# Two recurrent layers on one core: key blocks paired anew, row maxima sent through two queues, output division and values moved within a turn

## The chip, the cores and the metric

The kernel runs on one core of one Trainium2 chip. The metric is the device time of one launch in microseconds (us), lower is better. Each kernel is run several times; the median and the span of the runs are given.

## What is computed

The reference takes x of shape (4, 512, 512) and applies two gated layers. Cut to what matters here:

```python
xn = _layernorm(x)
s = _L0_attn_ref(xn, wq, wk, wv, wo)        # causal attention, 32 query heads of 16, 8 key heads, rope
g = _silu(_L0_ffn_ref(xn, ...))             # 2 of 8 experts: mean of relu(x W_e + b_e) of the chosen two
x = x + s * g
xn = _layernorm(x)
s = _L1_attn_ref(xn, ...)                   # S4: a 512-tap kernel from 64 states, causal convolution
g = _silu(_L1_ffn_ref(xn, ...))             # a linear layer with block-scaled weights
return x + s * g
```

The attention is a softmax over the keys up to each query: scores = q k / 4, masked above the diagonal, minus their maximum, exponentiated, times v, divided by the row's sum, then the product with `wo`.

## The kernel before, in words

The program has three stages, each written by hand in the order in which every engine runs it, with semaphores between the engines. Stage A (to about 105 us) normalizes, projects q, k and v, turns them and writes high and low parts of the turned q and k to HBM. Stage C (from about 671 us) is the second layer. The change lies in stage B, attention and experts together.

Stage B runs 32 **turns**, one for each pair (b, h) of 4 batches and 8 groups (a group is one key head with its four query heads). A turn works on two groups at once: the second pass of its own group, and the first pass of the next group.

- First pass, `scores_1` (L1358): scores with queries on the partitions, ten steps n of 512 columns or less in three banks. For each, VectorE adds the mask and takes the maximum of every row (`maxima`, L1179). Step n of `scores_1` waits until the maxima of step n-3 are taken. After the tenth step VectorE writes the negated maxima as two parts (`maxima_parts`, L1192 and L1194), TensorE turns them (`turn_maxima`, L1393), VectorE copies them out of the bank (`maxima_rows`, L1202), and SyncE sends them with two DMAs into rows of `qt` beside the queries (`maximum_rows`, L1085), one for each half of the heads (s = 0, 1).
- Second pass, `scores_2` (L1380 and L1383): scores with keys on the partitions, the maximum subtracted by those rows. The causal triangle of 4 x 4 blocks of 128 has ten blocks (j, t), key block j against query block t. They go two at a time, for both halves of the heads, so ten steps. Where the two blocks of a pair share the key block, one matmul of 512 columns does both (L1380); otherwise there are two of 256 columns with different weights (L1383). ScalarE exponentiates each step (`exps`, L1283) from one of two banks, so step n waits for the exponential of step n-2. Step 0 waits for the rows of maxima in `qt`. GpSimd masks the diagonal blocks (`select`, L1103).
- `values` (L1407): key block j times v, in four quarters j = 0 to 3 of 8 matmuls each. Quarter j needs all exponentials of the blocks of j.
- The division: `rows_of` (L1212) turns the outputs on VectorE, which needs all four quarters; `normalise` (L1217, L1221) divides; every second turn `pair_rows` (L1229) turns them back for the projection.
- Between these, TensorE does the experts' tiles (`expert`, L1422 turns the gathered rows, L1434 and L1437 multiply) and the output projection of the batch before (`project`, L1450). Five **bursts** make a turn: a burst is steps n and n+1 of both passes. What follows them is in four pieces, `filler(0)` to `filler(3)`: a quarter each of a projection, of a second tile, or of a tile that is done late in the turn.

A table of tiles for each turn (MIDDLE, FIRST, LAST) says which tiles run in it. In turns h = 0 to 3 of batches 1 to 3 the fillers are a projection (I call these projection turns); in turns with two tiles they are the second one; in six turns from 180 us on (229, 324, 355, 450, 481 and 576 us) the only tile is done late in the fillers, so the bursts have no expert work between them (late turns).

VectorE's order in a turn is: the ten maxima, with the division of the group before behind maxima 1, 3 and 5 (`finish`); `maxima_parts`; `dve_s4`, pieces of the second layer's taps (L545 and others); `maxima_rows`; in the first two turns the routing of tokens to experts (`dve_route`, `dve_tokens`), whose result the first gather of rows (L1116) waits for. ScalarE's is: exponentials, the tile's copy (`expert_x`, L1290) and relu (`expert_y`, L1296), and the copy of the projected tile (`projected`, L1273) at the end of the turn. SyncE's is: the tile's store (L1516), `maximum_rows`, in odd turns the twelve loads of the next two groups (`load_stacks`, L1077 and L1078), more stores. After the last turn SyncE loads what stage C needs (`sp_c`, from L1585), and TensorE works out the taps (`pe_taps`, L650) in the fillers of turn (3, 7).

## Time and profile before

| | us |
|---|---|
| median of 3 runs | 762.63 (761.85 to 764.82) |
| the profiled execution, its own time | 762.54 |
| its span in the profile | 760.8 |
| outside the span | 1.7 |
| TensorE busy | 681.8 (90%) |
| VectorE busy | 531.4 (70%) |
| ScalarE busy | 303.0 (40%) |
| GpSimd busy | 251.9 (33%) |

The span is the profiled program from its first instruction to its last. A busy share is a sum over the three stages. Waits are read from a timeline: each row gives start and length in us, the engine, the line of the kernel, what is written and read, how many instructions were merged (xN), and in brackets the idle time of the engine before it with what ended it. The granted clock is TensorE's, 1.00 for 2.4 GHz and 0.50 for 1.2 GHz.

### The profile page before, as it was taken

How to read it: one execution, taken by the hardware profiler on the slowest of the kernel's cores; microseconds unless marked ns; L12 is line 12 of the kernel's file. 1: busy time of each engine (PE TensorE's matmuls, PEld its weight loads, DVE VectorE, ACT ScalarE, POOL GpSimd, SP SyncE). 2: the span in 40 equal slices, each digit the busy share in tenths (PEclk: the TensorE clock that was granted, in tenths of full speed). 3: DMA queues.
4: the chain of work that ended last, by engine and by line, in shares of the span. 5: the costliest groups of instructions: out<-in, count | busy, mean ns of one | idle time of the engine just before them, and what ended most of it. 6: DMA issues, size and time to landing. Idle time of an engine off the chain costs nothing. (4 is left out here: it accounts for less than half of the span.)

```text
span 760.8 us, 12565 instructions
## 1 busy us (share of the span) xinstructions
PE 681.8 (90%) x3653; PEld 377.5 (50%) x3679; DVE 531.4 (70%) x1775; ACT 303.0 (40%) x553; POOL 251.9 (33%) x419
## 2 busy tenths in 40 slices
PE   3999956749999999999999999999999978869997
PEld 2888843334444443444443444444444433358886
DVE  4799878877757666676665776657766573359994
ACT  4344313323435443355433444344443432235442
POOL 2765521352232322222231222322222214446630
PEclk9999975558999999999999999999998997879999
DMA  7487877851726425154362432624415218648851
GB/s 228 145 271 266 266 185 175 218 91 31 132 71 120 89 60 105 42 95 87 62 132 59 78 75 47 123 75 98 80 41 96 67 45 279 135 79 191 207 137 69
DMA packets 52813, 92.25 MB, mean 121 GB/s; under 512 B 7800, under 2 KB 20664, under 8 KB 52752
## 3 DMA queue, kind: packets, MB, share of 16 engines
q1 hardware_dynamic: 40800, 64.21, 35.5%
q0 software_dynamic: 6704, 18.62, 10.9%
q10 hardware_dynamic: 5248, 8.69, 3.6%
q8 instruction: 29, 0.48, 0.3%
q14 instruction: 32, 0.26, 0.1%
HBM read 61.53 MB, written 29.43 MB: 120 GB/s over the span
## 5 line engine op out<-in xcount | busy, mean ns | idle before, releaser
L1179 DVE CUSTOM_DVE_ANT_0 bank<-bank,cst 128x384 f32<-128x384 f32 (+3 forms) x512 | 236.3, 518 | 142.2 <-PE bank L1358 140.0
L1283 ACT ACTIVATE arena<-bank 128x512 f32<-128x512 f32 x320 | 176.3, 602 | 126.8 <-PE bank L1380 85.1
L1103 POOL TENSOR_SCALAR_AFFINE_SELECT arena<-arena 128x512 f32<-128x512 f32 x128 | 81.6, 637 | 360.7 <-ACT arena L1283 360.6
L1437 PE MATMUL bank<-w_e,arena 128*128 x312 | 158.0, 617 | 4.6 <-issue 2.6
L1358 PE MATMUL bank<-kt,qt 48*128 48x384 f32 (+3 forms) x512 | 136.6, 370 | 13.2 <-DVE arena L1179 11.4
L1358 PEld LDWEIGHTS bank<-kt,qt 48*128 48x128 f32 x512 | 82.2, 208 | 113.0 <-DVE arena L1179 84.3
L1407 PE MATMUL bank<-arena 128*32 128x512 f32 (+3 forms) x1024 | 103.1, 502 | 0.0
L1380 PE MATMUL bank<-qt,kt 50*128 50x512 f32 x192 | 81.2, 525 | 14.2 <-DMA qt<-arena 10.5
L1437 PEld LDWEIGHTS bank<-w_e,arena 128*128 128x128 f32 x312 | 51.9, 190 | 55.2 <-issue 54.1
L1179 DVE DVE_READ_ACCUMULATOR2_ANT arena<- 128x1 f32 x512 | 71.9, 140 | 0.0
L1296 ACT ACTIVATE arena<-bank 128x512 f32<-128x512 f32 x39 | 23.3, 597 | 114.1 <-PE bank L1437 114.1
L1450 PE MATMUL bank<-w_proj,arena 128*128 128x512 f32 x128 | 64.2, 635 | 4.1 <-DVE arena L631 4.1
L1383 PE MATMUL bank<-qt,kt 50*128 50x256 f32 x256 | 57.9, 351 | 0.2 <-ACT arena L1283 0.2
L1380 PEld LDWEIGHTS bank<-qt,kt 50*128 50x128 f32 x192 | 34.7, 197 | 28.8 <-DMA qt<-arena 18.3
L1116 POOL DMA_INDIRECT arena<-xn_rows,arena x39 | 38.8, 994 | 29.1 <-issue 20.7
L836 PE MATMUL bank<-proj_high,xh 128*128 128x512 f32 (+1 forms) x128 | 46.9, 367 | 0.0
L836 PE MATMUL bank<-proj_high,xl 128*128 128x512 f32 (+1 forms) x128 | 44.3, 346 | 0.0
L836 PE MATMUL bank<-proj_low,xh 128*128 128x512 f32 (+1 forms) x128 | 44.2, 345 | 0.0
L1273 ACT COPY s_tok<-bank 128x512 f32<-128x512 f32 x16 | 9.4, 586 | 84.3 <-PE bank L1450 84.3
L1383 PEld LDWEIGHTS bank<-qt,kt 50*128 50x128 f32 x256 | 41.4, 217 | 2.6 <-issue 1.7
L698 POOL TENSOR_TENSOR s_tok<-arena 128x256 f32<-128x256 f32 (+1 forms) x64 | 33.9, 562 | 22.8 <-DVE arena L454 22.8
L1450 PEld LDWEIGHTS bank<-w_proj,arena 128*128 128x128 f32 x128 | 23.2, 197 | 35.1 <-issue 30.2
(162 smaller groups left out, 983.1 us busy)
## 6 DMA issues: line engine op xcount, KB each, us to landing
qt<-turned_parts SPq DMA_DIRECT2D x96, 128.0 KB, 4.9
turned_parts<-qk_parts SPq DMA_DIRECT2D x8, 1280.0 KB, 6.9
expert_rows<-arena SPq DMA_DIRECT2D x39, 256.0 KB, 2.0
w_e<-in_L_ffn_W_e ACTq DMA_DIRECT2D x8, 1024.0 KB, 7.2
kt<-turned_parts SPq DMA_DIRECT2D x96, 64.0 KB, 4.8
arena<-in_L_attn_x SPq DMA_DIRECT2D x16, 256.0 KB, 4.4
xn_rows<-arena SPq DMA_DIRECT2D x16, 256.0 KB, 2.8
w_e<-in_L_attn_x SPq DMA_DIRECT2D x16, 256.0 KB, 3.7
```

The costliest lines, as they stand in the source:

```text
L698: i = g.tensor_tensor(o[:, :, :, c, :], xc[:, :, :, c, :], xs[:, :, :, 1 - c, :], op)
L836: i = t.matmul(out[u % 2][:, 0:n], x[:, u % 2, k, :], w[part][:, k, :], start=(k == 0 and x is xh and part == 0), stop=(k == KB - 1 and pa ...
L1103: g.affine_select(out=diag, in_=diag, compare_op=ALU.is_ge, fill=0.0, base=0, pattern=[[0, 2], [0, HALF], [1, P]], channel_multiplier=-1). ...
L1116: e.indirect_dma_start(xg[:, m % 2, :], None, xn_d, bass.IndirectOffsetOnAxis(ap=tok_b[:, m % 2, :], axis=0))\
L1179: i = v.tensor_tensor_reduce(out=part, in0=part, in1=const("mask")[:, S - w:], scale=1.0, scalar=LOWEST, op0=ALU.add, op1=ALU.max, accum_o ...
L1283: a.activation(pt[:, s, 2 * i:2 * i + 2].rearrange("p c r q -> p (c r q)"), bank[2 + s], ACT.Exp, scale=HD ** -0.5)\
L1358: i = t.matmul(S1_BANK[n % 3][:, at:at + w], qt[rows, h // 2 % 2, h % 2, x if r is None else r, q * P:w], kt[rows, h // 2 % 2, h % 2, 0:w] ...
L1380: i = t.matmul(bank[2 + s], keys(j), queries[:, q:q + 2], start=True, stop=True)
L1383: i = t.matmul(bank[2 + s][:, x * HALF * P:(x + 1) * HALF * P], keys(j), queries[:, q], start=(x == 0), stop=True, skip_group_check=True)
L1407: i = t.matmul(bank[4][VW * r:VW * (r + 1), j * P:], vb[:, j, h, :], pt[:, r // HALF, at:at + TPB - j, r % HALF, :], start=(j == 0), stop= ...
L1437: i = t.matmul(bank[7], xgt[:, k, :], w_e[:, ex[b * MPB + m], k, :], start=False, stop=(k == KB - 1))
L1450: i = t.matmul(bank[to_bank or 7], ot[:, (b * PAIRS + k) % (PAIRS + 1), u, :], wo[:, k, :], start=(k == 0), stop=(k == KB - 1))
```

## The change

Four edits, all in stage B.

1. The ten blocks are paired by a table (`PAIRED`) in place of their order. Four of five pairs now share a key block; only ((1,3),(3,3)) does not. The exponentials write to the two places of a pair with a stride. Quarter 1 of the values now needs the last pair's exponentials, quarter 2 those of the fourth pair.
2. `maximum_rows` sends one half from SyncE and the other from ScalarE, where it stands behind the ten exponentials of the turn.
3. On VectorE, `maxima_rows` stands ahead of `dve_s4`, and the division of a group stands at the end of its own turn, behind both, in place of between the next turn's maxima. In turn (0, 0) it stands ahead of the routing, in turn (0, 1) behind it.
4. On TensorE, quarters 1 to 3 of the values stand together behind `filler(0)`, `filler(1)` and the turning of the maxima. The second tile's transposes move from behind the fifth burst to behind the fourth, its copy on ScalarE from behind the tenth exponential to behind the eighth.

```diff
+PAIRED = [((0, 0), (0, 1)), ((0, 2), (0, 3)), ((1, 1), (1, 2)), ((2, 2), (2, 3)), ((1, 3), (3, 3))]
...
-        VALUES_AFTER = [max(n for n in range(NJ) if (j, TPB - 1) in BLOCKS[n // 2 * 2:n // 2 * 2 + 2]) + 1 for j in range(TPB)]
+        VALUES_AFTER = [max(n for n in range(NJ) for t in range(j, TPB) if (j, t) in PAIRED[n // 2]) + 1 for j in range(TPB)]
...
-        def maximum_rows(e, b, h):
+        def maximum_rows(e, b, h, s):
 
             e.wait_ge(b_me, nth_of(1, b, h, 1))
-            for s in range(2):
-                at = 64 * s + ROWS
-                e.dma_start(qt[at:at + 2, h // 2 % 2, h % 2].bitcast(F32), m_rows[8 * TPB // 2 * s:8 * TPB // 2 * (s + 1), :]).then_inc(b_mr, 16)
+            at = 64 * s + ROWS
+            e.dma_start(qt[at:at + 2, h // 2 % 2, h % 2].bitcast(F32), m_rows[8 * TPB // 2 * s:8 * TPB // 2 * (s + 1), :]).then_inc(b_mr, 16)
...
                     for n in range(NJ):
                         if h + 1 < NG or more:
                             maxima(e, *next_group(b, h, 1), n)
-                        finish(b, h - 1, n)
                     if h + 1 < NG or more:
                         maxima_parts(e, st, *next_group(b, h, 1))
-                    dve_s4(e, st, b, h)
                     if h + 1 < NG or more:
                         maxima_rows(e, *next_group(b, h, 1))
+                    dve_s4(e, st, b, h)
+                    if due(b) or h != 1:
+                        finish(b, h)
                     if not due(b) and h < 2:
                         dve_route(e, st, h)
                     if not due(b) and h == 1:
                         dve_tokens(e, st)
+                        finish(b, h)
...
-                if due(at := nth_of(4, b, h, BLOCKS[2 * i + 1][0] - 3)):
+                if due(at := nth_of(4, b, h, PAIRED[i][1][0] - 3)):
                     e.wait_ge(b_pv, at)
-                a.activation(pt[:, s, 2 * i:2 * i + 2].rearrange("p c r q -> p (c r q)"), bank[2 + s], ACT.Exp, scale=HD ** -0.5)\
-                    .then_inc(b_e, 1)
+                first, second = (BLOCKS.index(block) for block in PAIRED[i])
+                a.activation(pt[:, s, first:second + 1:second - first].rearrange("p c r q -> p c (r q)"),
+                             bank[2 + s].rearrange("p (c x) -> p c x", c=2), ACT.Exp, scale=HD ** -0.5).then_inc(b_e, 1)
...
-                    if second is not None:
-                        expert_x(b, second)
+                        if n == Y_AT and second is not None:
+                            expert_x(b, second)
+                    if h + 1 < NG or more:
+                        maximum_rows(e, *next_group(b, h, 1), 1)
...
-                    if second is not None:
-                        expert(b, h, second, 0)
-                    values(b, h, 1)
+                            if second is not None:
+                                expert(b, h, second, 0)
                     filler(0)
+                    filler(1)
                     if following:
                         turn_maxima(*following)
-                    values(b, h, 2)
-                    values(b, h, 3)
-                    for k in range(1, 4):
-                        filler(k)
+                    for j in range(1, TPB):
+                        values(b, h, j)
+                    filler(2)
+                    filler(3)
```

The order of the instructions shows two of the moves. On TensorE, the end of turn (2, 0) before: the last scores of the second pass are `bank<-qt,kt`, the values `bank<-arena`, the projection `bank<-w_proj,arena`, the turned maxima `bank<-cst,m_parts`, the first pass `bank<-kt,qt`.

```order
L1383 MATMUL bank<-qt,kt 128x256 x2
L1407 MATMUL bank<-arena 32x384 x4
L1450 MATMUL bank<-w_proj,arena 128x512
L1393 MATMUL bank<-cst,m_parts 32x128
L1407 MATMUL bank<-arena 32x256 x4
L1407 MATMUL bank<-arena 32x128 x4
L1450 MATMUL bank<-w_proj,arena 128x512 x3
L1358 MATMUL bank<-kt,qt 128x512
```

The same place in the changed kernel:

```order
L1380 MATMUL bank<-qt,kt 128x256 x2
L1447 MATMUL bank<-w_proj,arena 128x512 x2
L1390 MATMUL bank<-cst,m_parts 32x128
L1404 MATMUL bank<-arena 32x384 x4
L1404 MATMUL bank<-arena 32x256 x4
L1404 MATMUL bank<-arena 32x128 x4
L1447 MATMUL bank<-w_proj,arena 128x512 x2
L1355 MATMUL bank<-kt,qt 128x512
```

Quarter 1 of the values went behind the turned maxima, and a second quarter of the projection came ahead of them. On VectorE, the end of turn (2, 3) before: `m_parts` are the maxima's parts, `arena<-arena 128x64` is `dve_s4`, `COPY arena<-bank 32x128` is `maxima_rows`, and the `ISA` rows are the next turn's maxima.

```order
L1194 SCALAR_TENSOR_TENSOR m_parts<-arena,m_parts 128x2x8
L545 TENSOR_TENSOR arena<-arena 128x64 x3
L570 RECIPROCAL arena<-arena 128x64
L545 TENSOR_TENSOR arena<-arena 128x64 x2
L1202 COPY arena<-bank 32x128
L1179 ISA bank,arena<-bank,cst 128x512
```

The same place in the changed kernel:

```order
L1194 SCALAR_TENSOR_TENSOR m_parts<-arena,m_parts 128x2x8
L1202 COPY arena<-bank 32x128
L546 TENSOR_TENSOR arena<-arena 128x64 x3
L571 RECIPROCAL arena<-arena 128x64
L546 TENSOR_TENSOR arena<-arena 128x64 x2
L1212 STREAM_TRANSPOSE arena<-bank 128x512
L1217 RECIPROCAL arena<-arena 128x16
L1221 TENSOR_TENSOR arena<-arena 128x16x16
L1229 STREAM_TRANSPOSE arena<-arena 128x512
L1179 ISA bank,arena<-bank,cst 128x512
```

The copy of the maxima comes ahead of the second layer's work, and the whole division of the turn's group stands ahead of the next turn's first maxima.

## Rows read from the trace of the kernel before

**Rows 1.** Timeline of TensorE, end of turn (2, 1), start of the next.

```profile
411.57 0.85 PE L1407 MATMUL bank<-arena 128*32 128x384 f32 x8
412.36 1.13 PE L1450 MATMUL bank<-w_proj,arena 128*128 128x512 f32 x2
413.64 0.28 PE L1393 MATMUL bank<-cst,m_parts 128*32 128x128 f32 x1 [0.16 <-DVE m_parts L1194]
413.85 0.86 PE L1407 MATMUL bank<-arena 128*32 128x256 f32 x16
414.64 2.84 PE L1450 MATMUL bank<-w_proj,arena 128*128 128x512 f32 x6
417.41 0.49 PE L1358 MATMUL bank<-kt,qt 48*128 48x512 f32 x1
418.58 0.60 PE L1380 MATMUL bank<-qt,kt 50*128 50x512 f32 x2 [0.67 <-DMA qt<-arena]
```

**Rows 2.** Timeline of SyncE's queue, ends of turns (2, 1) and (2, 3).

```profile
414.27 1.26 SPq L1085 DMA_DIRECT2D qt<-arena  x2
...
448.21 1.26 SPq L1085 DMA_DIRECT2D qt<-arena  x2
```

**Rows 3.** Waits of the second pass at L1380, both of TensorE's engines, 181 to 612 us.

```profile
  DMA qt<-arena: 13.5, 25
```

**Rows 4.** Timeline of TensorE, end of turn (2, 3), where `dve_s4` is long.

```profile
446.16 0.28 PE L1393 MATMUL bank<-cst,m_parts 128*32 128x128 f32 x1 [0.16 <-DVE m_parts L1194]
...
450.83 0.60 PE L1380 MATMUL bank<-qt,kt 50*128 50x512 f32 x2 [0.40 <-DMA qt<-arena]
```

**Rows 5.** Timeline of ScalarE, start of turn (2, 2).

```profile
417.52 0.58 ACT L1273 COPY s_tok<-bank 128x512 f32<-128x512 f32 x1 [4.94 <-PE bank L1450]
```

**Rows 6.** Timeline of TensorE, third and fourth burst of turn (2, 1), what follows each.

```profile
406.37 0.44 PE L1358 MATMUL bank<-kt,qt 48*128 48x384 f32 x1
...
407.08 1.12 PE L1437 MATMUL bank<-w_e,arena 128*128 x2
408.14 0.44 PE L1358 MATMUL bank<-kt,qt 48*128 48x384 f32 x1
...
408.85 1.06 PE L1407 MATMUL bank<-arena 128*32 128x512 f32 x8
```

**Rows 7.** Timeline of TensorE, late turn from 324 us.

```profile
329.65 0.44 PE L1358 MATMUL bank<-kt,qt 48*128 48x384 f32 x1 [0.47 <-DVE arena L1179]
...
330.09 1.73 PE L1407 MATMUL bank<-arena 128*32 128x512 f32 x8
```

**Rows 8.** Windows, right behind: length; busy PE, PEld, DVE, ACT, POOL; clock; DMA.

```profile
330.40:333.80 3.40, 3.40 (x24) 1.13 (x16) 3.27 (x16) 1.51 (x3) 0.64 (x1) 0.50 0.97 107
```

**Rows 9.** Timeline of VectorE, turn (0, 0): routing begins; the next maxima.

```profile
133.06 0.70 DVE L868 TENSOR_TENSOR arena<-arena 128x128 f32<-128x128 f32 x1
...
139.02 0.70 DVE L1179 CUSTOM_DVE_ANT_0 bank<-bank,cst 128x512 f32<-128x512 f32 x1
```

**Rows 10.** Timeline of TensorE, end of turn (0, 0), and turn (0, 2).

```profile
132.74 1.51 PE L1407 MATMUL bank<-arena 128*32 128x256 f32 x16
...
166.12 1.11 PE L1422 MATMUL bank<-cst,arena 128*128 128x128 f32 x4 [4.48 <-DMA arena<-xn_rows,arena]
```

**Rows 11.** Timeline of TensorE, turn (3, 7): second pass; taps.

```profile
627.15 0.67 PE L1380 MATMUL bank<-qt,kt 50*128 50x512 f32 x2 [4.05 <-DMA qt<-arena]
...
636.71 2.39 PE L650 MATMUL bank<-w_e,roots 128*128 128x512 f32 x4
```

**Rows 12.** Timeline of SyncE's queue: the load for the taps.

```profile
626.28 0.43 SPq L1585 DMA_DIRECT2D w_e<-in_dft  x1
```

**Rows 13.** DMA issues, KB each and median us to landing: the same load.

```profile
w_e<-in_dft SPq DMA_DIRECT2D x1, 2048.0 KB, 9.0
```

**Rows 14.** Timeline of VectorE: division of the last group, then stage C's scales.

```profile
639.95 0.72 DVE L1212 STREAM_TRANSPOSE arena<-bank 128x512 f32<-128x512 f32 x1 [14.02 <-PE bank L1407]
...
642.09 2.46 DVE L1674 TENSOR_TENSOR w_e<-w_e,arena 128x512 f32<-128x512 f32 x4
```

More of the change, by code:

```diff
@@ L1013, in build @@
         NLD = 2 * 3 * 2
-        SELECT_AFTER = [max(n for n in range(NJ) if (j, j) in BLOCKS[n // 2 * 2:n // 2 * 2 + 2]) + 1 for j in range(TPB)]
-        VALUES_AFTER = [max(n for n in range(NJ) if (j, TPB - 1) in BLOCKS[n // 2 * 2:n // 2 * 2 + 2]) + 1 for j in range(TPB)]
+        SELECT_AFTER = [max(n for n in range(NJ) if (j, j) in PAIRED[n // 2]) + 1 for j in range(TPB)]
+        VALUES_AFTER = [max(n for n in range(NJ) for t in range(j, TPB) if (j, t) in PAIRED[n // 2]) + 1 for j in range(TPB)]
         xb = bank[6].rearrange("p (k t) -> p k t", k=KB)
@@ L1229, in pair_rows, with finish @@
                 v.transpose(ot[:, (b * PAIRS + i) % (PAIRS + 1)].rearrange("p t f -> p (t f)"), o2.rearrange("p q c -> p (q c)")).then_inc(b_o2, 1)
-            def finish(b, h, n):
-                if h < 0 and not due(b):
-                    return
-                b, h = (b, h) if h >= 0 else (b - 1, NG - 1)
-                if n == ROWS_AT:
-                    rows_of(b, h)
-                if n == NORMALISE_AT:
-                    normalise(b, h)
-                if n == PAIR_AT and h % 2:
+            def finish(b, h):
+                rows_of(b, h)
+                normalise(b, h)
+                if h % 2:
                     pair_rows(b, h // 2)
@@ L1264, in dve_b @@
                 go(b, b + 1 < NB)
-            for n in (ROWS_AT, NORMALISE_AT, PAIR_AT):
-                finish(NB - 1, NG - 1, n)
             dve_scale(e)
@@ L1331, in build @@
         X_AT, Y_AT = 1, 7
-        ROWS_AT, NORMALISE_AT, PAIR_AT = 1, 3, 5
         def scores(e, n0, g1, g2):
@@ L1371, in scores_2 @@
             rows = slice(64 * s, 64 * s + ROWS + 2)
-            pair = BLOCKS[2 * i:2 * i + 2]
+            pair = PAIRED[i]
             queries = qt[rows, h // 2 % 2, h % 2].rearrange("p r (t q) -> p t r q", q=P)
@@ L1523, in go @@
                     if h + 1 < NG or more:
-                        maximum_rows(e, *next_group(b, h, 1))
+                        maximum_rows(e, *next_group(b, h, 1), 0)
                     if h % 2 and (h + 3 < NG or more):
@@ L1540, in go @@
                                  .then_inc(b_wo, 16)
-            maximum_rows(e, 0, 0)
+            for s in range(2):
+                maximum_rows(e, 0, 0, s)
             load_stacks(e, 0, 2)
```

## The prediction
> **What bounds the kernel now.** I read the shares first: TensorE is busy 90% of the span, VectorE 70%, ScalarE 40%. So I looked for what stops TensorE in stage B, 32 turns of about 16 us, with the timeline of one turn. The end of turn (2, 1) [rows 1] shows TensorE without a break except in two places. It waits 0.16 us for the maxima's parts before it turns them, and then, with the next turn's first-pass step issued at 417.41, it starts the second pass at 418.58, 1.17 us later, held by the DMA of the maxima's rows. A DMA that is not on any busy list therefore ends every turn. The chain to it is: turned maxima 413.64, two DMA issues of 0.63 us each from 414.27 [rows 2], landing and start at 418.58, which is 4.94 us behind the turned maxima, while TensorE has 3.77 us of work in between (413.64 to 417.41). The burst that holds the wait grows by all of it. Over 181 to 612 us this wait shows as 13.5 us of idle time in 25 of 27 turns [rows 3]. That is the prize and its bound.
>
> The wait has three parts. In turn (2, 3) the DMA issue comes 2.05 us behind the turned maxima (446.16 to 448.21) against 0.63 in turn (2, 1) [rows 1, 2, 4]: 1.42 us of `dve_s4` stands ahead of the copy. The second issue adds 0.63 us. From the end of the second issue, 449.47, to the start at 450.83 are 1.36 us of flight; in turn (2, 1), where the loads of the next stacks follow, the flight is 3.05 us (415.53 to 418.58).
>
> **Edit 3, first half: the copy ahead of `dve_s4`.** In six turns (2 and 3 of batches 1 and 2, 0 and 1 of batch 3) `dve_s4` delays the copy by about 1.4 us, in some others by less. In turn (2, 3) the second pass starts 0.9 us behind the first (0.49 of its step, 0.40 idle) [rows 1, 4]. 1.42 us earlier, it does not wait. Six times 0.9 is 5.4 us of the 13.5.
>
> **Edit 2: two queues.** Where the issue binds, 0.63 us go; where the engines are loaded and both land together, little. With quarter 1 moved, TensorE's work between turned maxima and next turn stays 3.7 to 3.8 us: 0.85 more for quarter 1, 0.94 less for a quarter of a projection (2.84 us for three) [rows 1]. So of the other 8.1 us I leave 0.8 us each in two turns with the longest waits, the one in rows 1 among them. ScalarE takes a floor: its copy at the start of a turn ends 0.69 us behind TensorE's first step (417.41 to 418.10) [rows 1, 5], and the first exponential can't start sooner. A second pass 0.1 us late costs nothing for that, so a tenth in 19 turns is not won. Sum of both edits: 13.5 - 1.6 - 1.9 = **10.0 us** won. Bounds: 13.5 if all goes, 5.4 if the second queue brings nothing. What ScalarE pays, one issue of 0.63 us a turn, lies in its idle time behind the tenth exponential (4.94 us before the copy of rows 5); nothing waits for it there. The late relu and the projected copy queue behind this wait, but need TensorE's last filler, 2 us later.
>
> The Trainium skill, page "DMA: Bandwidth & Descriptors", section "Issuing engines are not separate DMA queues", says that issuing from several engines saves the issue time alone, since all run on the same 16 engines. By it the flight of 3.05 us stays; that is the second rival.
>
> **Edit 4.** In projection turns, TensorE now has two projection quarters (some 1.9 us by rows 1, and about 0.2 for the change of operand) ahead of the turned maxima, where it had 0.85 + 1.13 and a wait. The turned maxima stay in place, at the end of the fifth burst plus 2.05; the wait and one change of operand go: 0.15 us in 12 turns, **1.8 us** (0 to 3). In turns with a second tile the transposes only move within TensorE's work, the copy still lands before its matmuls; I cost it at nothing, covered by the fifth burst (0.7 us), else 0.3 us a turn in 13 turns.
>
> **Edit 3, second half: the division.** Transpose, reciprocal, product and, in odd turns, the second transpose take 2.14 us (639.95 to 642.09), without the last 1.5 [rows 14]. They leave the maxima. That matters in the six late turns, where bursts two to four follow each other: the fourth waits 0.47 us for VectorE at 329.65, right ahead of the values at 330.09 [rows 7]. ScalarE is nearly as tight there, so I take 0.5 us a turn, **3.0 us** (1 to 6). The division now waits for quarter 3, which ends about 1.8 us behind the turned maxima, and must be done when the next first step is (another 2.4 us, a filler pair and the step): 2.14 fits. Where `dve_s4` and the numerators are long, in turns (0, 2) and (0, 3), it ends late; I take **1.3 us lost** (0 to 2).
>
> It costs in turn (0, 0). There the division stands ahead of the routing, which starts at 133.06 and ends at 139.02 [rows 9]. Quarters 1 to 3 run from 132.74 at half clock; quarters 2 and 3 take 1.5 us [rows 10], quarter 1 as much (equal at full clock, rows 1). So quarter 3 ends at 135.7, the division at 137.2, and the routing is 4.1 us late. The next maxima win 1.3 us back without a division among them. The chain goes on to the token lists and the gather that TensorE waits 4.48 us for at 166.12 [rows 10]: **2.8 us lost** (1.5 to 4).
>
> **Edit 1.** The fourth burst loses two matmuls of a half each. The third burst has the same first pass and whole matmuls already: 0.71 us from 406.37 to 407.08; the fourth: 0.71 us from 408.14 to 408.85 [rows 6]. So pairing is worth **nothing**; bounds 0 and 0.1 us a turn.
>
> **The end.** Turn (3, 7) waits 4.05 us for the rows behind the last `dve_s4` [rows 11]. That goes, but the taps come next: they need a load issued at 626.28 that takes 9.0 us [rows 12, 13]. The issue comes 2.1 us earlier at most, as it stands behind the last tile's relu, so it lands at 633.2. Then two tap quarters (2.3 us each at half clock) and three of values (1.5 to 3) run before the division: 639.3 to 640.8 against 639.95 [rows 11, 14]. **Nothing** won (2.7 won to 0.9 lost).
>
> **Sum.** -10.0 - 1.8 - 3.0 + 1.3 + 2.8 = -10.7. The profiled execution took 762.54 us, 0.1 under the median; 762.5 - 10.7 = **751.8 us**. All terms at their bounds give about 738 to 760.
>
> **The rivals.**
> - *The clock.* Behind each late turn's bursts the granted clock falls to 0.50 for 3.4 us or 6.8, six times; one of them is in [rows 8]. Values at half clock take 1.73 against 1.06 [rows 6, 7], and the burst and quarter 1 behind them lose as much: 1.5 to 2 us a fall. If shorter waits keep 2.4 GHz there, 8 us more: 744. For it: TensorE was idle in the bursts just before. Against: they stay limited by ScalarE.
> - *The engines, not the issue.* The rows land no earlier through two queues, by the flight of 3.05 us in rows 1. Then 13.5 falls to 5.4 us and 751.8 becomes 756.4.
> - *VectorE late at every turn.* The division, waiting for quarter 3 through the masks, ends behind the next turn's first step. The fourth first-pass step needs maximum 0, so I estimate that the first 0.4 us of lateness is free, about half a burst [rows 6]; each further us costs one in 31 turns. At 1 us late (1.2 us over my estimate) it costs 31 x 0.6 = 18 us: 770, slower. For it: the margin in odd turns is under 0.3 us. Against: all durations in it are measured, and the even turns have 1 us to spare without the second transpose.
> - *The end and the start go badly*, each at its bound, and the late turns win nothing: 759 to 761.
>
> **Chances.** Forecast 0.53, clock 0.17, engines 0.17, VectorE 0.07, the last 0.06. About 0.5%, 3.8 us, is what a measurement can tell. Faster: 0.85; same: 0.09; slower: 0.06. The range, 743 to 760, leaves out the slower case, and the far end of the clock's.
>
> **What would show it.** Right: the copy 0.3 us behind the turned maxima everywhere; one row DMA on each queue, 0.6 us each; second pass under 0.2 us behind the first step in most turns; the fourth burst 0.7 us as before; routing beginning near 137 us. Wrong: VectorE's division ending behind the next first step, or TensorE waiting for maxima in the second burst; rows landing 4.9 us behind the turned maxima still.

## The result and the profile after

| | before | after |
|---|---|---|
| median, us | 763.1 (761.85 to 764.82) | 774.14 (771.31 to 778.96) |
| profiled execution: own time, span | 762.54, 760.8 | 778.96, 777.2 |
| mean granted clock | 0.917 | 0.903 |

The changed kernel takes 1.0145 times as long, interval [1.0108, 1.0183]. The forecast was 751.8 us, with a range of 743 to 760 and 0.06 for slower. The profiled execution after is the longest of its four, so what is read from it is set against experiments that change one thing each. In what follows a ratio is to the kernel before as run beside it. The ratio of the run with the routing first leaves out two of its six executions, which were in a slower state of the chip, and so stands for 745 us where the median of all six is 749.05.

First, where the time went. The windows view, cut where the maxima are turned at the end of turn (0, 3) and at the end of turn (3, 5), the same two steps in both kernels; the columns are length, busy time (instructions) of PE, PEld, DVE, ACT and POOL, granted clock, DMA share and GB/s. Before:

```profile
0.00:193.21 193.21, 149.73 (x848) 107.24 (x850) 151.08 (x436) 64.38 (x119) 82.98 (x169) 0.81 0.66 186
193.21:603.33 410.12, 393.68 (x2155) 174.58 (x2176) 276.44 (x1088) 180.99 (x340) 106.69 (x175) 0.97 0.42 83
603.33:760.80 157.47, 138.39 (x654) 95.64 (x653) 103.85 (x253) 57.61 (x94) 62.19 (x75) 0.91 0.54 141
```

After:

```profile
0.00:196.30 196.30, 149.16 (x836) 107.35 (x836) 150.52 (x433) 64.43 (x119) 83.24 (x169) 0.82 0.65 183
196.30:619.66 423.36, 399.38 (x2125) 181.39 (x2124) 289.17 (x1088) 180.52 (x340) 109.00 (x175) 0.94 0.41 80
619.66:777.20 157.54, 137.83 (x657) 95.12 (x656) 105.88 (x254) 57.62 (x94) 61.71 (x75) 0.91 0.54 141
```

The end is unchanged (+0.1 us), the start lost 3.1, and the 26 turns between lost 13.2. There TensorE's matmuls stood idle for 24.0 us (423.36 - 399.38) against 16.4, and were busy 5.7 us longer although they were fewer; the granted clock was 0.94 against 0.97.

What ended the idle time, from the waits view of this stretch (total us, times, longest). Before, for matmuls alone:

```profile
PE bank L1380 <- DMA qt<-arena: 3.8, 8, 0.7
PE bank L1422 <- DMA arena<-xn_rows,arena: 0.5, 1, 0.5
```

After (L1377 is the second pass, L1419 the transposes of a tile's gathered rows):

```profile
PE bank L1377 <- DMA qt<-arena: 11.9, 11, 2.4
PE bank L1419 <- DMA arena<-xn_rows,arena: 10.0, 6, 2.3
```

[rows 3] has 13.5 us in 25 places for the first of these. It adds the waits of two queues of TensorE, 3.8 us of the matmuls in 8 places and 9.7 us of the weight loads that run ahead of them in 17. The 8 turns of the matmuls are among the 17 of the weight loads, so the same waits are in the sum twice; what TensorE lost to the rows before the change is 3.8 us in 8 turns.

By the matmuls' count the wait that the change was to remove grew threefold (by [rows 3]'s count, which has 16.0 us of weight loads more, it doubled), and a new one stands beside it: TensorE now waits for gathered rows. Of the 22.0 us of both, 20.1 follow the turned maxima of the 13 odd turns, where SyncE issues the stack loads, and 2.0 those of the 13 even turns. One place of each kind. First the end of turn (2, 3) of after, which answers to [rows 2, 4], on TensorE, then on SyncE's queue:

```profile
457.96 0.28 PE L1390 MATMUL bank<-cst,m_parts 128*32 128x128 f32 x1
458.18 1.50 PE L1404 MATMUL bank<-arena 128*32 128x384 f32 x24
459.61 1.99 PE L1447 MATMUL bank<-w_proj,arena 128*128 128x512 f32 x4
461.53 0.49 PE L1355 MATMUL bank<-kt,qt 48*128 48x512 f32 x1
463.91 0.60 PE L1377 MATMUL bank<-qt,kt 50*128 50x512 f32 x2 [1.89 <-DMA qt<-arena]
```

```profile
458.59 0.62 SPq L1085 DMA_DIRECT2D qt<-arena  x1
459.38 0.33 SPq L1078 DMA_DIRECT2D kt<-turned_parts  x1
459.74 0.62 SPq L1079 DMA_DIRECT2D qt<-turned_parts  x1
...
464.71 0.42 SPq L1079 DMA_DIRECT2D qt<-turned_parts  x1
```

Every step that the change controls went as meant: the copy is at once behind the turned maxima, the row DMA is issued 0.63 us behind them (ScalarE's half at 458.60), where [rows 2, 4] have 2.05 and then a second issue. But the second pass starts 5.95 us behind the turned maxima; before it was 4.67. From the row's issue to the start are 5.3 us. Right behind the row, SyncE issues the loads of the next stacks (`load_stacks`, every second turn), twelve of 64 and 128 KB, ten of them within these 5.3 us. They too start earlier than they did, since they queue behind the row: 1.4 us behind the turned maxima, where the same turn had 3.5 before (446.16 to 449.64) and turn (2, 1) had 2.1.

```profile
449.64 0.33 SPq L1077 DMA_DIRECT2D kt<-turned_parts  x1
```

The second kind, at the start of turn (2, 6), on TensorE and on GpSimd, which had issued the gather of these rows at 491.12, 0.6 us behind the turned maxima:

```profile
496.50 0.84 PE L1419 MATMUL bank<-cst,arena 128*128 128x128 f32 x4 [1.67 <-DMA arena<-xn_rows,arena]
```

```profile
491.12 1.20 POOL L1116 DMA_INDIRECT arena<-xn_rows,arena  x1 [0.75 <-POOL arena L1111]
```

The gather landed 5.3 us after its issue, at 496.46. In the kernel before, the same one was issued 0.1 us behind the turned maxima (477.64) and landed in 3.3 us. All six waits of this kind follow an odd turn, with the stack loads issued beside the gather, and these six gathers took 4.7 to 5.9 us.

What follows, by windows (columns as above): TensorE had full clock up to the wait, and behind it 1.2 GHz for 10.2 us, without a break in its work. Not all of that can be put to the wait: in the kernel before the clock fell in this turn too, for 3.4 us (487.4 to 490.8).

```profile
490.53:496.80 6.27, 4.60 (x37) 2.05 (x37) 4.54 (x11) 1.57 (x3) 3.01 (x4) 1.00 0.63 123
496.80:507.00 10.20, 10.20 (x40) 6.09 (x39) 6.52 (x30) 4.93 (x9) 2.11 (x5) 0.50 0.72 120
```

From these turned maxima to the next it took 17.2 us (490.53 to 507.71), and 14.6 in the kernel before:

```profile
477.56:492.16 14.60, 13.31 (x76) 6.10 (x76) 10.45 (x42) 6.53 (x12) 4.83 (x8) 0.88 0.78 136
```

In after's turn (3, 4), of the same kind, TensorE waited for nothing, and it took 12.1:

```profile
592.03:604.13 12.10, 12.10 (x76) 5.91 (x75) 10.65 (x41) 6.30 (x12) 3.90 (x6) 1.00 0.78 119
```

### The profile page after: what moved, and what is told of

It reads as the page before. It is cut to its first block and busy times, and to the rows that moved or that the text cites. A ratio compares the mean times of both kernels' runs of the same rounds, so it can differ in the third digit from the quotient of the medians.

```text
span 777.2 us, 12463 instructions
## 1 busy us (share of the span) xinstructions
PE 686.4 (88%) x3615; PEld 383.9 (49%) x3615; DVE 545.6 (70%) x1775; ACT 302.6 (39%) x553; POOL 253.9 (33%) x419
## 3 DMA queue, kind: packets, MB, share of 16 engines
q1 hardware_dynamic: 40242, 63.95, 34.2%
q0 software_dynamic: 6704, 18.62, 11.2%
## 5 line engine op out<-in xcount | busy, mean ns | idle before, releaser
L1434 PE MATMUL bank<-w_e,arena 128*128 x312 | 165.3, 642 | 0.0
L1355 PEld LDWEIGHTS bank<-kt,qt 48*128 48x128 f32 x512 | 84.2, 215 | 106.1 <-DVE arena L1179 58.0
L1377 PE MATMUL bank<-qt,kt 50*128 50x512 f32 x256 | 112.8, 531 | 16.0 <-DMA qt<-arena 13.6
L1404 PE MATMUL bank<-arena 128*32 128x512 f32 (+3 forms) x1024 | 92.6, 482 | 0.0
L1434 PEld LDWEIGHTS bank<-w_e,arena 128*128 128x128 f32 x312 | 56.1, 202 | 59.0 <-issue 56.2
L1377 PEld LDWEIGHTS bank<-qt,kt 50*128 50x128 f32 x256 | 48.3, 204 | 28.2 <-DMA qt<-arena 19.1
L1116 POOL DMA_INDIRECT arena<-xn_rows,arena x39 | 41.1, 1054 | 29.1 <-issue 20.8
L1404 PEld LDWEIGHTS bank<-arena 128*32 128x32 f32 x1024 | 27.7, 114 | 33.4 <-issue 25.5
L1212 DVE STREAM_TRANSPOSE arena<-bank 128x512 f32<-128x512 f32 x32 | 22.9, 717 | 26.3 <-PE bank L1404 25.5
L1419 PE MATMUL bank<-cst,arena 128*128 128x128 f32 x156 | 26.3, 293 | 15.1 <-DMA arena<-xn_rows,arena 15.0
```

The costliest lines, as they stand in the source:

```text
L1116: e.indirect_dma_start(xg[:, m % 2, :], None, xn_d, bass.IndirectOffsetOnAxis(ap=tok_b[:, m % 2, :], axis=0))\
L1355: i = t.matmul(S1_BANK[n % 3][:, at:at + w], qt[rows, h // 2 % 2, h % 2, x if r is None else r, q * P:w], kt[rows, h // 2 % 2, h % 2, 0:w] ...
L1377: i = t.matmul(bank[2 + s], keys(j), queries[:, q:q + 2], start=True, stop=True)
L1404: i = t.matmul(bank[4][VW * r:VW * (r + 1), j * P:], vb[:, j, h, :], pt[:, r // HALF, at:at + TPB - j, r % HALF, :], start=(j == 0), stop= ...
L1434: i = t.matmul(bank[7], xgt[:, k, :], w_e[:, ex[b * MPB + m], k, :], start=False, stop=(k == KB - 1))
```

## The experiments

**Theory L** after the first look: the loads of the stacks, released earlier, are in flight with the rows and the gathers, and delay both; TensorE stops, and its clock falls. **Rival Q**: the rows' two halves delay each other, or the second queue costs something. **Rival T**: the second tile's earlier place causes the waits for gathered rows, and these the loss. **Rival V**: VectorE's late division. In the first four expectations Q stands for L and Q together (the rows meet the loads, on ScalarE's queue above all).

### The changed kernel with both halves from SyncE

```diff
                     if h + 1 < NG or more:
-                        maximum_rows(e, *next_group(b, h, 1), 0)
+                        for s in range(2):
+                            maximum_rows(e, *next_group(b, h, 1), s)
```

and without ScalarE's issue.

> The changed kernel with both halves of the maxima's rows sent from SyncE again, ahead of the stack loads. Theory Q (the half on ScalarE's queue meets the stack loads, which now start 0.6 us sooner): in stack-loading turns the rows land within 3 to 4 us of the copy in place of 4.8 to 5.9, second pass late by 1 us at most, total 760 to 766. Theory T (the gathers are late since two ScalarE copies stand ahead of the last exponentials, and TensorE waits for their rows): total 770 to 775, the waits for gathered rows unchanged at about 15 us. Theory V (division at the turn's end holds up the first maxima): 772 to 776.

Measured: 783.19 us (777.4 to 784.95), ratio to before 1.0242 [1.0184, 1.0301]. All three forecasts were too low. The second queue is a gain of 7 to 9 us inside the changed kernel (the intervals of the two ratios just part), not its fault: rival Q falls.

### The changed kernel with the loads held behind the rows

```diff
                     if h % 2 and (h + 3 < NG or more):
+                        e.wait_ge(b_mr, nth_of(32, *next_group(b, h, 1), 32))
                         load_stacks(e, *next_group(b, h, 3))
```

> The changed kernel, two queues kept, but SyncE issues the stack loads only once both halves of the rows have landed. Theory Q: the rows land 2.0 to 2.4 us behind the copy in every turn and the gathers within 3.5 us of issue, waits for gathered rows fall from 15 us to under 3, total 750 to 758. Theory T: the rows as Q says, but X0 waits stay over 8 us, 764 to 770. Theory V: 770 or more.

Measured: **749.29 us** (744.18 to 754.22), ratio 0.9811 [0.9747, 0.9874]. One wait on SyncE turns 1.5% slower into 1.9% faster, and V falls. The same stretch, cut at the same steps, and its waits:

```profile
196.75:585.67 388.92, 383.38 (x2125) 173.71 (x2124) 288.21 (x1088) 179.05 (x340) 109.76 (x175) 0.99 0.43 88
```

```profile
PE bank L1377 <- DMA qt<-arena: 2.5, 10, 0.5
PE bank L1419 <- DMA arena<-xn_rows,arena: 0.5, 2, 0.3
```

Against after: 34.4 us shorter, of which 18.4 are idle time (24.0 to 5.5) and 16.0 the same 2125 matmuls in 383.4 us rather than 399.4. So the clock took nearly as much as the waits. The two traces overstate both: this one is of the shortest of four executions (744.18), that of after of the longest, and the medians are 24.9 us apart. That the clock has a part is clear without them: it was 0.903 to 0.913 in the four executions of after and 0.918 to 0.933 in these. The end of turn (2, 3) again, TensorE and SyncE's queue:

```profile
438.68 0.28 PE L1390 MATMUL bank<-cst,m_parts 128*32 128x128 f32 x1
...
443.05 0.60 PE L1377 MATMUL bank<-qt,kt 50*128 50x512 f32 x2 [0.32 <-DMA qt<-arena]
```

```profile
439.30 0.62 SPq L1085 DMA_DIRECT2D qt<-arena  x1
443.02 0.32 SPq L1078 DMA_DIRECT2D kt<-turned_parts  x1
```

From issue to start 3.75 us, against 5.3. SyncE's first load is now issued as soon as both halves have landed, so its time tells the landing, here 3.72 us after the row's issue. The DMA engines' share of those stretches, issue to start (first after, second this kernel; columns as in the windows above):

```profile
458.60:463.90 5.30, 3.42 (x29) 1.31 (x21) 4.30 (x12) 0.59 (x1) 0.96 (x1) 1.00 0.71 130
```

```profile
439.30:443.05 3.75, 3.43 (x30) 1.32 (x22) 3.44 (x10) 0.58 (x1) 0.96 (x1) 1.00 0.25 74
```

### The changed kernel with the second tile back in its old place

```diff
                         if n == Y_AT and first is not None and not late:
                             expert_y(b, first)
-                        if n == Y_AT and second is not None:
-                            expert_x(b, second)
+                    if second is not None:
+                        expert_x(b, second)
```

and on TensorE `expert(b, h, second, 0)` likewise, behind the fifth burst.

> The changed kernel with the second tile's transposes and copy at their old places (behind the fifth burst, behind the tenth exponential). Theory T: the two gathers of such turns go out 0.6 us sooner, waits for gathered rows fall from 15 us to 5, total 762 to 768. Theory Q: rows in the projection turns land as late as in the changed kernel, the gathers gain little, total 770 to 776. Theory V: 772 to 776.

Measured: 780.52 us (777.64 to 785.2), ratio 1.0226 [1.0167, 1.0285]. All forecasts were too low again. No wait for gathered rows is left, yet the kernel is no faster than after (6 us slower by the medians, with intervals that overlap): rival T falls. The waits of the second pass are longer still, and TensorE waits for the tile's copy:

```profile
PE bank L1377 <- DMA qt<-arena: 13.9, 6, 3.2
PE bank L1434 <- ACT arena L1286: 6.8, 9, 0.8
```

### The kernel before with two queues

The `maximum_rows` of the change, its second half issued by ScalarE behind `expert_x`, nothing else.

```diff
+                    if h + 1 < NG or more:
+                        maximum_rows(e, *next_group(b, h, 1), 1)
                     if late:
                         expert_y(b, first)
```

> The kernel before with the two queues alone. Theory Q: slower than before, 764 to 772, rows landing 4.8 to 5.9 us behind the copy in stack-loading turns. Theories T and V: a gain of 1 to 5 us, 758 to 762, since the issue of 0.6 us goes.

Measured: 767.98 us (766.51 to 770.24), ratio 1.0059 [1.001, 1.0108]. Alone, the second queue loses 4 us, just clear of noise. The loads, which stood behind both issues, now stand behind one.

### The kernel before with the loads held

The same wait ahead of `load_stacks` as above, in the kernel before.

```diff
+                        e.wait_ge(b_mr, nth_of(32, *next_group(b, h, 1), 32))
                         load_stacks(e, *next_group(b, h, 3))
```

> The kernel before, and SyncE waits for both landings of the maxima's rows before it issues the twelve stack loads of odd turns. Theory L (the stack loads, issued about 2.1 us behind the turned maxima, meet the rows in flight; in the kernel before that costs TensorE little more than 7 us, since its waits ahead of the next scores sum to 14.7 us over turns 4 to 30): with the loads held the waits fall to 8 to 10 us in sum, 755 to 761 us. Rival (holding the loads is worth some 25 us by itself in any kernel, as it was in the changed one, for a reason that has nothing to do with the change's earlier issues): 735 to 745 us. Rival (the loads then come too late for their own use, or nothing hangs on them): 763 to 770 us.

Measured: 760.95 us (758.12 to 766.24), ratio 0.998 [0.9948, 1.0013]. So the loads are nearly harmless there, and the 25 us in the changed kernel are a matter of the two together. At the end of turn (2, 3) the second pass starts 4.67 us behind the turned maxima with the loads held and without; at that of turn (2, 1), where the loads had followed 2.1 us behind them, it starts at 4.33 in place of 4.94. In the kernel before other things fill or end the same gap: the rows leave behind `dve_s4` and a second issue, and TensorE waits for VectorE as well.

```profile
PE bank L1358 <- DVE arena L1179: 3.5, 6, 0.8
PE bank L1380 <- DMA qt<-arena: 3.0, 8, 0.5
```

### Loads held, one queue

Both edits, on the changed kernel.

```diff
+                        for s in range(2):
+                            maximum_rows(e, *next_group(b, h, 1), s)
...
+                        e.wait_ge(b_mr, nth_of(32, *next_group(b, h, 1), 32))
```

> The changed kernel with the loads held behind the rows, and both halves of the rows issued by SyncE as before. By the changed kernel with loads held and two queues (749.3 us) and my term for the second queue (1.26 us of one issue in each of 31 turns, of which TensorE saw nearly all): theory Q (the second queue saves its 1.2 us a turn once the loads are out of its way): 30 to 40 us more than 749, of which the clock is a part, so 765 to 785 us if the rows wait for each other as they did in the one-queue run (30.2 us of waits); with the term alone, 27 turns x 0.7 us, 760 to 768 us. Rival (the whole loss was the loads, the queue of the rows matters little): 747 to 754 us.

Measured: 761.63 us (754.23 to 764.8), ratio 0.9951 [0.9914, 0.9988]. That is what the term alone would give. Against 749.3 the second queue is worth 12 us, and the loads held are worth 22 us with one queue too (783.2 to 761.6). The order within one queue is therefore not how the loads do harm: here the rows always stand ahead of them on the same queue. The second issue of 0.63 us shows as waits in 17 turns, 3.3 us more in sum than with two queues, and the rest of the 12 us is other idle time and clock:

```profile
PE bank L1375 <- DMA qt<-arena: 5.8, 17, 0.5
```

### Loads held, the division back between the maxima

```diff
                     for n in range(NJ):
                         if h + 1 < NG or more:
                             maxima(e, *next_group(b, h, 1), n)
+                        finish(b, h - 1, n)
```

with the `finish` of the kernel before.

> The changed kernel with the loads held, and the division of the outputs (rows, reciprocals, pairs) put back between the maxima of the next group, where the kernel before has it. Theory (the prediction's term: the division between the maxima cost 3.0 us in late turns and 1.8 us in projection turns, and something of the dve_s4 turns; with the loads held these terms are the gain): 754 to 760 us against 749.3. Rival (VectorE's place is free, since TensorE waits for the maxima only in the late turns): 748 to 752 us. Rival (the division behind the maxima delays the expert numerators more than it gains): under 747 us.

Measured: 755.49 us (752.89 to 759.68), ratio 0.9911 [0.988, 0.9942]: 6 us slower than with the division behind the maxima, as the theory had it. TensorE waits for VectorE again, which it did once, for 0.5 us, in the kernel with the loads held:

```profile
PE bank L1360 <- DVE arena L1179: 4.0, 6, 0.9
```

### The loads held longer

```diff
+                        e.wait_ge(b_e, nth_of(NJ, *next_group(b, h, 1), 4))
                         load_stacks(e, *next_group(b, h, 3))
```

> The changed kernel, with the twelve stack loads of odd turns held until the fourth exponential of the next turn is done, some 7 us behind the maxima, when the gathers of the second tile's rows have landed as well. Theory L (rows and gathers both pay for the loads beside them): gathers land within 4 us again, TensorE's waits for gathered rows fall below the 1.0 us of the run with loads held behind the rows, and the time is at or a little below it, 743 to 750 us. Rival (gathers aren't disturbed by loads, rows alone are): within 0.3% of 749.3. Rival (the loads collide with the next turn's gathers, weights or rows instead): 752 us or more, with waits at other places.

Measured: 770.33 us (767.55 to 773.55), ratio 1.0087 [1.0061, 1.0113]. The last rival was right. SyncE now stands in this wait while a store and the next turn's loads queue behind it, and the first pass waits for the stacks themselves:

```profile
PE bank L1355 <- DMA qt<-turned_parts: 8.6, 4, 2.7
```

So the loads have a window: behind the rows, but not 7 us behind the maxima.

### Loads held, the copy back behind `dve_s4`

```diff
+                    dve_s4(e, st, b, h)
                     if h + 1 < NG or more:
                         maxima_rows(e, *next_group(b, h, 1))
-                    dve_s4(e, st, b, h)
```

> The changed kernel with the loads held behind the rows, and the copy of the turned maxima put back behind the expert step dve_s4, as the kernel before has it. The term of the prediction: in six turns the copy stood 0.9 us or so behind dve_s4, 5.4 us in sum. Theory (the term was right): 749.3 + 4 to 6 us, 753 to 756 us. Rival (TensorE has other work in those turns, so the copy's place is free): 748 to 751 us. Rival (the wait stops TensorE and its clock falls, at more than the wait itself): 757 us or more.

Measured: 764.66 us (759.45 to 769.66), ratio 1.0029 [0.9999, 1.0059]: 15 us for the place of one copy of 0.28 us, which is the last rival's range. (`dve_s4` is the second layer's taps and no expert step.) It isn't only the six turns that I counted. A turn in which `dve_s4` is short, on VectorE, and what TensorE then does:

```profile
351.72 0.42 DVE L546 TENSOR_TENSOR w_proj<-w_proj 128x256 f32<-128x256 f32 x1
352.17 0.42 DVE L584 TENSOR_REDUCE arena<-w_proj 128x4 f32<-128x256 f32 x1
352.63 0.28 DVE L1202 COPY arena<-bank 32x128 f32<-32x128 f32 x1
```

```profile
356.32 0.60 PE L1377 MATMUL bank<-qt,kt 50*128 50x512 f32 x2 [0.41 <-DMA qt<-arena]
```

The copy comes 0.45 us later than behind the turned maxima, the row is issued at 352.94, and the second pass waits. Why so little matters so much is seen on SyncE's queue, where the first load tells the landing. End of turn (2, 5) with the copy in its new place, turned maxima at 468.56:

```profile
469.19 0.62 SPq L1085 DMA_DIRECT2D qt<-arena  x1
471.40 0.32 SPq L1078 DMA_DIRECT2D kt<-turned_parts  x1
```

With the copy put back, turned maxima at 474.97:

```profile
476.05 0.62 SPq L1085 DMA_DIRECT2D qt<-arena  x1
479.47 0.33 SPq L1078 DMA_DIRECT2D kt<-turned_parts  x1
```

Issued 0.45 us later, the rows land 1.65 us later, 4.50 behind the turned maxima in place of 2.85. In the 13 odd turns from (0, 3) to (3, 3), with the loads held and both edits in, the landing is 2.8 to 3.0 us behind the turned maxima in seven turns and 4.0 to 4.3 in six; with the copy back, or with one queue, it is 4.0 to 4.6 in all thirteen, although the issues lie between 0.6 and 2.1. Up to about 3.5 us a landing costs TensorE nothing, since it has work until then. What the rows wait for beyond their issue is not shown; the gather of a tile's rows is issued 0.6 us behind the turned maxima in all these turns, and lands at 4 to 5 us where the trace has it.

The waits in all are 7.2 us in 17 turns against 2.5 in 10, and TensorE's busy time for the same work grows from 383.4 to 395.3 us:

```profile
194.27:600.50 406.23, 395.25 (x2126) 179.04 (x2125) 290.45 (x1089) 180.14 (x340) 107.16 (x175) 0.97 0.42 84
```

### Loads held, the blocks paired as before

```diff
-PAIRED = [((0, 0), (0, 1)), ((0, 2), (0, 3)), ((1, 1), (1, 2)), ((2, 2), (2, 3)), ((1, 3), (3, 3))]
+PAIRED = [tuple(BLOCKS[n:n + 2]) for n in range(0, len(BLOCKS), 2)]
```

> The changed kernel with the loads held, and the score blocks paired as the kernel before pairs them (two of the five pairs with two keys, rather than one). Theory (bursts are bound by the exponentials that empty the banks, burst 4 took 0.71 us in both kernels, so the pairing is worth nothing): 748 to 751 us. Rival (one weight load and one start fewer in each of 64 bursts of 32 turns is worth 0.1 us each): 754 to 757 us. Rival (values 1 to 3 wait for later exponentials with the new order of blocks, so that the old one gains): 745 to 747 us.

Measured: 749.64 us (745.87 to 754.9), ratio 0.9835 [0.9791, 0.9878]. No difference within the 0.5% that these runs resolve: the pairing is worth nothing that can be measured. Its trace has 390.5 us of busy matmuls in the stretch (2178 of them) against 383.4.

### Loads held, routing ahead of the division in turn (0, 0)

```diff
                     if not due(b) and h < 2:
                         dve_route(e, st, h)
+                    if not due(b) and h == 0:
+                        finish(b, h)
```

> The changed kernel with the loads held, and in turn (0,0) the expert routing ahead of the division of the outputs, as in turn (0,1). The term of the prediction was +2.8 us for routing behind the division in turn (0,0). Theory (the term was right: the gathers and so the first expert rows come 2.5 us earlier): 746 to 747.5 us. Rival (the division then comes late for the values of the next turn, and gives it back): 749 to 752 us. Rival (the wait only moves, since the gathered rows bound that turn by their flight): 748.5 to 750 us.

Measured: 749.05 us (739.84 to 754.06), ratio 0.9769 [0.9712, 0.9825]. The times don't tell it from the kernel with the loads held; the ratios' intervals overlap. The trace shows the term, though: the first gathered rows' transposes start 34.2 us behind the maxima turned at the end of turn (0, 0) (133.16 to 167.31), 35.9 with the division first (134.43 to 170.29), and 33.7 in the kernel before.

```profile
167.31 1.12 PE L1421 MATMUL bank<-cst,arena 128*128 128x128 f32 x4 [4.42 <-DMA arena<-xn_rows,arena]
```

### Loads held, the second tile back

> The changed kernel with the loads held, and the second tile's transposes, their copy by ScalarE and so the next gather at the places of the kernel before. Theory (the tile's new place costs only where its gather meets the loads, which are now held; it takes nothing from the path otherwise): 748 to 752 us, with waits for gathered rows at 0. Rival (the new place brings the values 1 to 3 together and keeps TensorE's clock up): 755 to 762 us. Rival (the new place is still a loss, since gathers are issued 0.5 us later): 744 to 747 us.

The edit is that of the third experiment, on the kernel with the loads held. Measured: 754.85 us (753.03 to 756.62), ratio 0.9904 [0.9869, 0.994], at the lower edge of the first rival. The new place of the tile is a gain of some 6 us with the loads held, as it was with them free (774.1 against 780.5); each time the intervals just meet, so it is the two together that speak for it. What TensorE waits for with the tile back is the tile's copy, 6.8 us in 9 places in both kernels, and nowhere with the new place. With the tile back, holding the loads gains 26 us although no gathered row is ever waited for. So the rows of the maxima alone can carry the loss. How it divides between rows and gathers in the changed kernel itself isn't shown; its trace has 11.9 us of waits for the one and 10.0 for the other.

## Why the prediction was wrong

**What failed is one assumption under Edit 2 and Edit 3, that the flight stays.** I subtracted time from the issue of the rows and left their flight alone, 1.36 us in turn (2, 3) and 3.05 in turn (2, 1), "where the loads of the next stacks follow", with 0.8 us in two turns for the loads. But the loads follow in turn (2, 3) too, at 449.64; what differs is that they came late there. They are issued by the same engine right behind the row, so everything that makes the row earlier makes them earlier, and the work that covers the flight did not grow. From the end of the row's issue to the start, turn (2, 3) went from 1.36 us to 4.70. I asked of VectorE and ScalarE what queues behind a moved step, but not of SyncE, where the next instructions are those loads. The last of my signs of being wrong came, and worse than I had it: rows used 5.95 us behind the turned maxima. Nor does the flight stay with the loads held: issued 1.4 us earlier, the rows of turn (2, 3) are used 0.3 us earlier.

**The prize was read wrong too.** The 13.5 us of [rows 3] count the same waits on two queues; the matmuls lost 3.8 us in 8 turns, not 13.5 in 25. Six times 0.9 us took in 0.49 us of a step in which TensorE works. With the loads held the wait for the rows went from 3.8 to 2.5 us, so the term of -10.0 us did not come in that form even there.

**The cited rule.** With the loads free, the rows were slow through one queue (783.2 us) and through two (774.1). The sentence of the Trainium skill ("DMA: Bandwidth & Descriptors", section "Issuing engines are not separate DMA queues") that DMAs of all engines run on the same 16 engines and "interleave with each other" agrees with that. I had used the section only for a flight that stays at 3.05 us, which it does not state and which did not hold: at the end of turn (2, 1) it was 3.80 us in after.

**Copy ahead of `dve_s4`, 5.4 us:** 15 us in the kernel with the loads held. I counted six turns with 1.4 us; the rest, with 0.45 us, also cross the line between a landing near 2.9 us and one above 4.

**Second queue:** 12 us there, against the 4.6 that was left for it beside `dve_s4`. These sizes don't add up: putting back one edit alone costs 15, 12, 6 and 6 us (copy, queue, division, tile), 39 in sum, while the kernel before with the loads held is only 11.7 us slower than the changed one with them held. The copy and the queue need each other, as the landings show.

**The projection turns, 1.8 us,** weren't isolated; the wait for the maxima's parts at L1393, 2.2 us in 12 places before, is 0.3 us in one place after, which is about the term. **The second tile at nothing** ("the copy still lands before its matmuls") was wrong in both directions: some 6 us gained, since with the tile in its old place TensorE waits 6.8 us for the copy, and with the loads free a new wait of 10.0 us for gathered rows. In the turn shown, the gather was issued 0.5 us later than before and the loads 0.7 us earlier, so that they met. I had not looked at when the gathers land.

**The division, 3.0 us:** right place, size 6 us. The rival that VectorE ends late each turn fell. At the end of turn (2, 3) of after, the division's last transpose does end behind the first step, by 0.55 us (461.86 + 0.71 against 461.53 + 0.49), but in the whole stretch of the held kernel TensorE waits for the maxima once, for 0.5 us.

**Turn (0, 0), 2.8 us lost:** routing begins at 137.67 and the first gathered transposes stand 35.6 us behind the turned maxima at the end of turn (0, 0) (133.10 to 168.71), 33.7 before (132.42 to 166.12). Lost 1.9; of the 3.1 us up to turn (0, 4) the rest isn't assigned.

```profile
168.71 1.11 PE L1419 MATMUL bank<-cst,arena 128*128 128x128 f32 x4 [4.43 <-DMA arena<-xn_rows,arena]
```

**Pairing and the end, nothing:** right. The rows of the last group don't hold TensorE any more, and the taps come next, as foreseen: the load is issued at 640.28, the division starts 16.5 us later than in [rows 14], which is the whole kernel's difference of 16.4.

```profile
639.18 0.49 PE L1377 MATMUL bank<-qt,kt 50*128 50x512 f32 x2
...
648.75 6.20 PE L651 MATMUL bank<-w_e,roots 128*128 128x512 f32 x8 [2.33 <-issue]
```

**The clock** was a rival in one direction, a gain of 8 us. It worked in both. With the loads free it took 5.7 us more busy time than before; with them held it gave 10.3 (393.7 to 383.4), of which the fewer matmuls of the pairing may be up to 7.1 (390.5 with the old pairs). The held kernel comes close to the forecast, 749.3 for 751.8, and that is luck: of its 10.9 us less idle time only 1.3 are waits for the rows, some 5 are waits for VectorE's maxima and their parts and 1.7 for the tile's copy, and the rest of the gain is busy time.

**The sum and its bounds.** The terms at their bounds, added again, give 736 to 763 us, and 767 with the tile's 0.3 us in 13 turns, not 738 to 760. The measured 774 us lies outside these too.

**Open.** Whether the loads delay a row at the DMA engines they share, or in reading or writing the same memory, wasn't tried. Nor is it shown why with the loads held and a DMA share of 0.25 the rows need 3.4 to 3.7 us in six odd turns and 2.2 to 2.4 in the other seven. In the six, GpSimd's gather instruction beside them takes 1.0 us, in the seven 1.2, so which of the two comes first may decide it; but with the second tile back, two turns with 1.0 us land early all the same. A run without the gather would tell.

## What to carry to other kernels

When a small transfer on the critical path is moved earlier, look at what its queue issues next: bulk loads behind it come earlier too, and can take back more than was won. Make the bulk wait for the small transfer's landing, one wait on the issuing engine, but release it soon enough for its own reader (here, 7 us behind the maxima was too late). A wait of TensorE in a stage that is nearly always busy can cost more than its length: against the trace with the loads held, four traces with the same matmuls had 5.4, 5.6, 18.4 and 22.1 us more idle time, and 11.9, 3.1, 16.0 and 17.7 us more busy time. Before adding up waits, see that each is counted once: weight loads and matmuls of TensorE wait for the same thing side by side. And when edits feed one threshold, as the copy and the queue do here, their worth alone and together differs.

## What the runs showed of the hardware

- 16 KB of rows in two DMAs took 3.75 us from issue to use beside a gather, and 5.3 us with loads of 64 and 128 KB issued behind it as well (DMA share 0.25 and 0.71).
- The small transfer's landing was not a fixed time behind its issue: issued 0.63 us behind the turned maxima it landed at 2.85, issued at 1.08 it landed at 4.50 (loads held, same turn, two kernels).
- A gather of rows landed in 3.3 us where the stack loads began 2.1 us behind the turned maxima (turn (2, 6), kernel before), and in 5.3 us where they began at 1.4.
- A stop of 1.67 us at full clock was followed by 10.2 us at 1.2 GHz, in which TensorE did not pause. Over 26 turns the same 2125 matmuls (one more in the second trace) took 383.4, 395.3 or 399.4 us by the waits around them (5.5, 11.0 and 24.0 us of idle time).
- The sum of idle time doesn't set it: 11.0 and 11.2 us went with 395.3 and 386.5 us of busy time (the copy back, the tile back).
